# Last feed-forward rebuilt and interleaved with the second attention; its chunks on VectorE

## What is computed

```python
# second layer's attention (phasor memory), cut
ao = (gelu(off_in @ hop_w1 + hop_b1) @ hop_w2 + hop_b2).reshape(B, L, H, P + 1)
off_ph = center[:, :, :, None, :] + deltas[..., None] * 0.1
retrieved = (einsum('blpd,blhp->blhd', mem1_cos, qc) + einsum('blpd,blhp->blhd', mem1_sin, qs)) / sqrtP
gv = values[:, :, None, :] * gate[..., None]
kv_ret = (kv_cos * key_cos[..., None] + kv_sin * key_sin[..., None]).sum(axis=2)
# second layer's FFN: six experts of 64-64-64-64, the two best per token, weighted
rh = relu(features @ router_w1 + router_b1)
top_w, top_i = jax.lax.top_k(softmax(rh @ router_w2 + router_b2), 2)
routing_weights = softmax(top_w)
h1 = relu(einsum('bsd,edh->bseh', features, expert_w1) + expert_b1)
h2 = relu(einsum('bseh,ehf->bsef', h1, expert_w2) + expert_b2)
expert_out = einsum('bsef,efo->bseo', h2, expert_w3) + expert_b3
combined = sum over the two chosen experts of weight * expert_out
```

## Time and profile before

| | value |
|---|---|
| runs (us) | 1465.36, 1470.60, 1472.48; median 1470.6 |
| profiled execution | 1465.17 us, its span 1463.1 us |
| busy share PE / DVE / ACT / POOL | 80% / 60% / 42% / 42% |
| first attention | about 90 to 820 us |
| first FFN | about 820 to 940 us |
| second attention | about 950 to 1321 us |
| last FFN | 1321 to 1463 us |

### The profile page before, as it was taken

How to read it: one execution, slowest core, us unless ns; L and a number is a source line. 1 busy time by engine, 2 the same in 40 slices (tenths; PEclk the granted TensorE clock), 3 DMA queues, 4 the chain that set the end, 5 groups by cost and what they waited for, 6 DMA issues and landing times.

```text
span 1463.1 us, 26112 instructions
## 1 busy us (share of the span) xinstructions
PE 1167.1 (80%) x9805; PEld 769.0 (53%) x9805; DVE 875.2 (60%) x1807; ACT 614.5 (42%) x1249; POOL 608.9 (42%) x1193
## 2 busy tenths in 40 slices
PE   5579999999999999999999937305476674837995
PEld 3345565666666666666666623103264554734663
DVE  3434655655565565655656323146889888732998
ACT  1224555555554545545455413103352524213552
POOL 3201444734545445454554631478534635440000
PEclk9768999999999999999999967657667586666998
DMA  3100000000000000000000011211000000000000
GB/s 79 24 1 1 2 3 2 5 5 2 4 2 2 2 2 3 2 2 2 2 2 2 2 29 61 66 16 17 1 1 0 1 0 1 12 0 0 12 16 16
DMA packets 31369, 14.78 MB, mean 10 GB/s; under 512 B 27522, under 2 KB 28642, under 8 KB 31245
## 3 DMA queue, kind: packets, MB, share of 16 engines
q1 hardware_dynamic: 26637, 11.21, 3.3%
q0 software_dynamic: 4608, 1.91, 1.4%
HBM read 6.72 MB, written 7.27 MB: 10 GB/s over the span
## 4 chain that ended last, share of the span: by engine, by line
PE 63%; DVE 24%; POOL 6%; issue 4%; DMA 2%; ACT 1%; SPq 0%; POOLq 0%; DVEq 0%; ACTq 0%
PE psum L700 20%; PE psum L681 10%; PE psum L609 8%; PE psum L672 7%; PE psum L656 3%; DVE arena L1965 3%; PE psum L594 2%; DVE arena L1964 2%; DVE arena L1959 2%; PE psum L519 1%; POOL lnst L1089 1%; PE psum L614 1%; PE psum L751 1%; PE psum L764 1%; DVE lnst L1613 1%
## 5 line engine op out<-in xcount | busy, mean ns | idle before, releaser
L1355 ACT ACTIVATE arena<-psum 125x500 f32<-125x500 f32 x576 | 306.8, 585 | 342.9 <-PE psum L681 342.9
L1643 DVE TENSOR_REDUCE arena<-psum 125x1 f32<-125x500 f32 x384 | 242.6, 673 | 208.7 <-PE psum L609 208.5
L609 PE MATMUL psum<-arena 32*125 32x500 f32 (+1 forms) x1536 | 324.9, 520 | 0.6 <-ACT arena L1346 0.6
L700 PE MATMUL psum<-arena,XN 125*64 125x250 f32 x2304 | 308.6, 388 | 0.2 <-ACT arena L1355 0.2
L681 PE MATMUL psum<-arena 32*125 32x250 f32 x2304 | 293.9, 371 | 0.0
L681 PEld LDWEIGHTS psum<-arena 32*125 32x125 f32 x2304 | 216.0, 183 | 12.1 <-issue 1.4
L700 PEld LDWEIGHTS psum<-arena,XN 125*64 125x64 f32 x2304 | 140.6, 137 | 123.3 <-issue 78.0
L1646 DVE TENSOR_REDUCE arena<-psum 125x2 f32<-125x500 f32 x192 | 121.4, 674 | 72.6 <-PE psum L609 72.6
L609 PEld LDWEIGHTS psum<-arena 32*125 32x125 f32 x1536 | 128.6, 184 | 3.5 <-issue 2.1
L672 PE MATMUL psum<-arena,onesb 3*125 3x500 bf16 x576 | 123.3, 422 | 5.3 <-DMA arena<-arena 5.3
L1118 POOL TENSOR_SCALAR arena<-arena 125x4 bf16<-125x4 f32 x96 | 21.9, 229 | 217.3 <-DVE arena L1651 215.5
(11 more groups left out here) (327 smaller groups left out, 2079.0 us busy)
## 6 DMA issues: line engine op xcount, KB each, us to landing
arena<-arena SPq DMA_DIRECT2D x192, 1.5 KB
expert_in<-XN SPq DMA_DIRECT2D x8, 256.0 KB, 4.8
arena<-expert_in SPq DMA_DIRECT2D x4, 512.0 KB, 5.1
expert_out<-arena SPq DMA_DIRECT2D x4, 512.0 KB, 2.7
out<-H SPq DMA_DIRECT2D x8, 187.5 KB
expert_in<-XN,slot_in POOLq DMA_INDIRECT x48, 2.5
XN<-expert_out,slot_out POOLq DMA_INDIRECT x48, 3.9
arena<-in_L_ffn_w SPq DMA_DIRECT2D x2, 256.0 KB, 4.2
```

Source lines behind the costliest of these rows:

```text
L609: last = pe.matmul(ps[0:R, at_:at_ + hi - lo], QH[row:row + 32, b, g, j * R:(j + 1) * R], KH[row:row + 32, b, g, lo:hi], start=True, stop= ...
L700: last = pe.matmul(ctx_bank[64 * h2:64 * h2 + 64, 0:THIRD], XN[:, p, c, a, :], PR[:, x % 4, h2, i * THIRD:(i + 1) * THIRD], start=(c == 0) ...
L1355: act.activation(PR[:, x % 4, h2, :], st_bank[(2 * x + h2) % 3][0:R, 0:2 * THIRD], ACT.Exp)\
L1643: dve.reduce_max(MX[:, q % 2, 0, 2 * h2 + tile:2 * h2 + tile + 1], ps[0:R, 0:2 * THIRD], AX)\
```

## The change

It has five parts.

1. *The FFN by steps.* 24 steps k = (p, th, ep), both sequences in each. Layer 1 is two matmuls of 64 rows on the two halves of the array (`tile_position`), layer 2 two full ones. The gates are spread over partitions by a matmul with the 0/1 matrix `SEL` from transposed gates `GT`, and DVE multiplies the second layer's activations by them. Layer 3 has `e3w` as stationary operand, 64 output columns for each sequence, and sums all six experts in one bank together with the bias, weighted by the gates (`b3r`). ACT copies the sum, PE transposes it, DVE adds it to `H`; SP stores each half, 16 stores in place of 8.
2. *Its place.* `ffn_events` puts `router`, `logit`, `gates` of pair p into events 20, 21, 22 for p = 0, 26 to 28 for p = 1, 32 to 34 for p = 2, and two steps into each of events 23 to 25, 29 to 31 and 35 to 37. Pair 3's comes behind. Choices and routes are made for each pair, on 72 values of a partition in place of 288.
3. *Chunks on DVE.* POOL's part goes. DVE forms all four products in two instructions of 1024, then difference and sum, two halving additions in place of the two sums over heads, and the six of 128. ACT scales values and keys, eight instructions of 64 a chunk, after a new wait on `rg`; PE's wait on `ff` goes.
4. *First attention's start.* `before` now also holds the six scores of unit 1, and `max_step` is moved by three up to k = 11; the shift of unit 1 is at step 0.
5. *Small.* `room` is in event 16; POOL makes `SEL` and zeroes `GP`, `b3r` there; the broadcast of the third bias goes.

```diff
@@ plan
+        def ffn_events(x):
+            heads = 0
+            while head1 and heads < (1 if x is not None else 2):
+                kind, p = head1[0]
+                if x is not None and x <= NJ * (p + 1) + 13:
+                    break
+                events.append(head1.pop(0))
...
+            while body1 and (x is None or done < PER):
+                k = body1[0][1]
+                p = steps1[min(k, len(steps1) - 1)][0]
+                now = [g for g in given if g[0:2] == ("gates", p)]
+                if x is not None and (not now or now[0][2] == x):
+                    break
...
+            if EARLY:
+                ffn_events(x)
+        ffn_events(None)
@@ first attention
-            return (k - 3) // 2 if k < 15 else k - 9
+            return (k - 6) // 2 if k < 12 else k - 9
-        shift_at = {min(max_step(3 * q + 2) + 2, 3 * q - 1): q for q in range(1, NQ)}
+        shift_at = {min(max_step(3 * q + 2) + 2, 3 * q - 1) if q > 1 else 0: q for q in range(1, NQ)}
-        before += [("score", 0, i) for i in range(6)] + [("shift", 0)]
+        before += [("score", 0, i) for i in range(6)] + [("score", 1, i) for i in range(4)] + [("shift", 0)]
+        before += [("score", 1, i) for i in range(4, 6)]
@@ TensorE
+            def layer1(k):
+                for a in range(2):
+                    r = slice(64 * a, 64 * a + 64)
+                    ps, done = take(pe, ("l1", k, a))
+                    pe.matmul(ps[:, 0:HALF], e1w[r, ep, :], XT[r, cols], start=True, stop=True,
+                              tile_position=(64 * a, 0)).then_inc(done, 1)
+            def gate_spread(k):
+                emptied(pe, ("gt", p, th))
+                for a in range(2):
...
+                    pe.matmul(ps[:, 0:HALF], SEL[r, ep].rearrange("r e d -> r (e d)"),
+                              GT[r, p % 2, th * HALF:(th + 1) * HALF], start=True, stop=True,
+                              tile_position=(64 * a, 0)).then_inc(done, 1)
+            def layer2(k):
+                for a in range(2):
+                    emptied(pe, ("l1", k, a))
+                    ps, done = take(pe, ("l2", k, a))
+                    pe.matmul(ps[:, 0:HALF], e2w[:, ep, :], H1[(2 * k + a) % 4], start=True, stop=True)\
+                        .then_inc(done, 1)
+            def layer3(n):
...
+                for a in range(2):
+                    pe.matmul(ps[64 * a:64 * a + 64, 0:HALF], b3r[:, a, :], GT[:, p % 2, th * HALF:(th + 1) * HALF],
+                              start=True, stop=False, tile_position=(0, 64 * a))
+                for ep in range(3):
+                    for a in range(2):
+                        last = pe.matmul(ps[64 * a:64 * a + 64, 0:HALF], e3w[:, ep, :], H2[6 * (n % 2) + 2 * ep + a],
+                                         start=False, stop=(ep == 2), tile_position=(0, 64 * a))
+                elif kind == "step":
+                    if x < len(steps1):
+                        layer1(x)
+                    if 1 <= x <= len(steps1):
+                        gate_spread(x - 1)
+                        layer2(x - 1)
+                    if x >= 4 and x % 3 == 1:
+                        layer3(x // 3 - 1)
+                    if x >= 5 and x % 3 == 2:
+                        turned(x // 3 - 1)
@@ ScalarE, chunk
+                act.wait_ge(S["rg"], p + 1)
+                act.wait_ge(S["gate"], p + 1)
+                for n in range(4):
+                    v = CV[:, tiles.start + n // 2, n % 2, 1, :]
+                    act.activation(v, v, ACT.Copy, scale=GA[:, 0, 4 * q + n:4 * q + n + 1])
                 act.wait_ge(S["prod"], q + 1)
-                act.wait_ge(S["vsum"], q + 1)
+                for n in range(4):
...
+                                   ACT.Copy, scale=GA[:, 5, 4 * q + n:4 * q + n + 1])
@@ VectorE, chunk
+                for i in range(2):
+                    w = WA[:, i:i + 2, 16 * q:16 * q + 16].unsqueeze(3).to_broadcast([R, 2, 16, PP])
+                    last = dve.tensor_tensor(t4[:, 2 * i:2 * i + 2], cs, w, ALU.mult)
+                last.then_inc(S["prod"], 1)
                 dve.wait_ge(S["prod"], q + 1)
-                link(dve.tensor_tensor(p0, p0, p1, ALU.subtract))
-                dve.reduce_sum(UV[:, 0], PT[:, 0].rearrange("r g h p -> r g p h"), AX)
-                dve.wait_ge(S["vsum"], q + 1)
-                dve.reduce_sum(UV[:, 1], PT[:, 2].rearrange("r g h p -> r g p h"), AX).then_inc(S["uv"], 1)
+                dve.tensor_tensor(t4[:, 0], t4[:, 0], t4[:, 1], ALU.subtract)
+                link(dve.tensor_tensor(t4[:, 2], t4[:, 2], t4[:, 3], ALU.add))
+                h4 = PT.rearrange("r (n i) g h p -> r n i g (h p)", i=2)[:, :, 0]
+                link(dve.tensor_tensor(h4[:, :, :, 0:64], h4[:, :, :, 0:64], h4[:, :, :, 64:128], ALU.add))
+                link(dve.tensor_tensor(UV, h4[:, :, :, 0:32], h4[:, :, :, 32:64], ALU.add))
@@ VectorE, FFN
+            def gated(k):
...
+                for a in range(2):
+                    emptied(dve, ("l2", k, a))
+                    g, done = filled(dve, ("gate", k, a))
...
+                    dve.tensor_tensor(H2[6 * (n % 2) + 2 * ep + a], H2R[(2 * k + a) % 4], g[:, 0:HALF], ALU.mult)\
+                       .then_inc(done, 1)
```

More of the change, by code:

```diff
@@ L885, in product, with router @@
                     last.then_inc(done, 1)
+            def router(p):
+                if p == 0:
+                    pe.wait_ge(S["w_late"], 16 * 11)
+                for th in range(2):
+                    emptied(pe, ("xt", 3, p, th))
+                for th in range(2):
+                    cols = slice(p * L + th * HALF, p * L + (th + 1) * HALF)
+                    ps, done = take(pe, ("rh", p, th))
+                    pe.matmul(ps[0:64, 0:HALF], W["rw1"], XT[:, cols], start=True, stop=True).then_inc(done, 1)
@@ L887, in _, with turned @@
+            def turned(n):
+                emptied(pe, ("l3", n))
+                ps, done = take(pe, ("yt", n))
+                for m in range(3):
+                    last = pe.transpose(ps[0:R, m * 128:(m + 1) * 128], YS[:, n % 2, m * R:(m + 1) * R], ident)
+                last.then_inc(done, 1)
             for event in events:
@@ L904, in _ @@
                     product(event[2])
[L907 to L917, removed]
@@ L950, in _ @@
-            NX = len(units)
-            for x in range(NX + 1):
-                if x < NX:
-                    layer1(x)
-                if x:
-                    layer2(x - 1)
-                    if x >= 6 and x % 3 == 0:
-                        layer3(*units[x - 6][0:3])
-            layer3(*units[NX - 3][0:3])
+                elif kind == "router":
+                    router(x)
+                elif kind == "logit":
+                    logit(x)
+                elif kind == "gates":
+                    gates(x)
+                elif kind == "step":
[8 more added lines that the diff above has]
+                        turned(x // 3 - 1)
@@ L1797, in weights @@
             def weights(p):
[L1799 removed]
+                wa = [WA[:, i, 48 * p:48 * p + 48] for i in (0, 1, 3, 2)]
                 dve.wait_ge(S["wexp"], p + 1)
@@ L1972 @@
+                elif kind == "logit":
+                    choices(x)
+                elif kind == "gates":
+                    route(x)
+                elif kind == "step":
+                    if 1 <= x <= len(steps1):
+                        gated(x - 1)
+                    if x >= 5 and x % 3 == 2:
+                        added(x // 3 - 1)
 _INS = ['x', 'L0_tok_conv_w', 'L0_tok_conv_b', 'L0_tok_bn_gamma', 'L0_tok_bn_beta', 'L0_tok_bn_mean',
```

418 lines of the change are left out of this document (237 added, 181 removed).

## The result

The changed kernel takes 1428.2 us (median of four, 1425.6 to 1430.4) against 1471.5 for the kernel before on the same chip: ratio 0.971, 95% interval 0.968 to 0.975, 43 us less. The prediction was 1428.0, range 1388 to 1462. The profiled execution took 1428.26 with a span of 1426.3.

The account below looks back on a forecast made before the run. DVE was taken to bound the second attention and last feed-forward, nothing the tail between. From 1465.2 us, less 8 (start), 28 (chunks) and 5 (event 20 to the end), came 1424; plus 4 for the median, 1428, range 1388 to 1462.

Parts of the forecast that it names:

- The bound of each part: DVE bounds the second attention and old last feed-forward, nothing bounds the tail; PE bounds the new feed-forward.
- Chunks, -28: Second attention: chunks moved wholly to DVE take 6.4 us each; 33 us less, of which 28 is counted.
- Start, -8: First attention's start: removing the stall and slow steps saves 8 us, bounds 0 and 12, and carries through.
- A step on PE, 4.07: New feed-forward: a block of three steps takes PE 12.2 us with eight changeovers, 4.07 a step, 98 us in all.
- The clock behind a head, 3 each: Behind the attention: the clock needs 3 us to come back after each head.
- The parts of the end: Event 20 to the end: 54 us (events 20 to 25), 94 (26 to 37), 51 (pair 3), together 199.
- Interleaving buys little: Feed-forward steps among attention events: event 20 to the end takes 199 us instead of 204, 5 less.
- Heads, 14 each: Behind the attention: a pair's router, logits, choices, route and transposes take 14 us with PE nearly idle.
- Rival 1: Behind the attention: heads hide, their 28 us and 9 of clock fall to a third, chunk gives 33; 1398, chance 0.22.
- Rival 2: Second attention: DVE's relief isn't the path's; chunk gains 5 to 15 us, start nothing; about 1450, chance 0.15.
- Rival 3: Feed-forward steps: the clock stays low; at half clock 98 us double, 1506 if 80% of steps run low; chance 0.08.
- Rival 4: Feed-forward on PE: paired half-array matmuls don't overlap, 50 us more, 1478; chance 0.05.

Follow-up runs that it names:

- the run with the small additions: The changed kernel with GpSimd's residual, bias, scale and offset work done for one group of 64 columns instead of twelve: 1412.3 us, ratio 0.961.
- The last experiment: Against the 1412.2 us kernel (heads ahead of layer norms, steps spread, gates later), DVE makes the gates directly behind the choices: 1400.7 us, ratio 0.953.
- the kernel with two steps earlier: Against the 1414.9 us kernel (heads ahead of layer norms, steps one to an event beside heads), steps start two events earlier: 1423.3 us, ratio 0.968.

## Why the prediction was right, and where it wasn't

- **The bound of each part** held. DVE bounds the second attention: with the chunk alone, chunk 11 starts 28 us earlier. The wait of PE on a chunk's last instruction is 31.9 us, no longer 42.8; I had it under 40.
- **Chunks, -28.** The free chunk was put at 6.4 (the terms as given add up to 6.3) and is 6.25. From chunk 0 to chunk 11 after has 201.0 us, before 226.5 by 1032.82 and 1259.28: -25.5. The step that failed is "nothing waits for what stays": what stays on POOL holds DVE, 7.2 us in this stretch by the run with the small additions. Together that is 32.7, the 33 that I had counted before I took 5 off for a late PE; the allowance was near in size and wrong in cause. I expected first and third chunk alike; the first of pairs 1 to 3 are 9.1 to 11.5 against 6.25. And 4.5 us of the gain are given back by the clock some 13 us behind chunk 11, which the prediction had only as a general remark on PE.
- **Start, -8.** Some 20 us ahead of chunk 0, at the same instruction of DVE (L1787 in before, at 1014.06; L1921 in after, at 1005.50), after is 8.6 us ahead. At chunk 0 it is 7.4, and by the run with the old start 7 to 9. The third step starts at 102.80, in front of the 103 I named. "No 0.50 behind it" is true of what follows; the first slow stretch, ahead of it, lasts longer than before.
- **A step on PE, 4.07.** At full clock a block of three takes 1368.77 - 1356.37 less 0.73 for six transposes of the layer norm = 11.7 us, 3.9 a step. The Trainium skill (TensorEngine Tiling (Array Packing), Key Properties) has a change of tiling mode drain the engine, which I charged with 0.15 to 0.2 each. Without any charge 10.7 was the sum, with it 12.2. That 11.7 lies between is in part luck, since the price of a unit was too low and the charge too high. Two groups of row pairs, with no change between them, start 0.73 apart (1356.37, 1357.10), where I had 0.63 a pair. Two full products take 1.46 with a change behind them (1357.83 to 1359.29) and 1.37 with transposes of the same mode behind them (1363.42 to 1364.79). So the trace agrees that a change costs something, but no more than 0.09 us there. The three transposes take 0.42 instead of 0.64.
- **The clock behind a head, 3 each.** No row stood behind this term. The first step behind the transposes of pairs 1 to 3 takes 3.7 to 4.4 us (1308.71 to 1312.43, 1352.21 to 1356.37, 1389.10 to 1393.53) instead of 2.92 by the starts at 1312.43 and 1315.35, and the six transposes themselves 1.44 instead of 0.8: 1.5 to 2.2 us a head.
- **The parts of the end.** Event 20 to the end is 1426.3 - 1226.4 = 199.9 us; I had 199. Inside, 61 instead of 54 (events 20 to 25), 90 instead of 94, 48.6 instead of 51. That the sum is right to 1 us is luck. In the first part 34.6 us pass before the first step (I had 32) and 26.6 with the steps (I had 22). The clock has a share in it: it is 0.57 from 1240 to 1270, and I costed steps at full clock. PE also stands 9 us at the waits of head 0 (3.60 and 5.42). What each is worth no run shows.
- **"Interleaving buys little."** This step failed. It is worth 13.5 to 14.7 us, since the feed-forward behind everything is no faster than the old one (4 us slower by the traces). My sum held because I set new parts against the old total of 204, without asking what the rewritten feed-forward would be on its own. In the run with the old feed-forward event 20 to the end is 208.9 us, not 204: the 4.5 of the clock are in it. So the feed-forward's share is 9 to 11 instead of 5, and the chunk's is 22 to 25 instead of 28; these are the two errors that cancel, and that they do is luck.
- **Heads, 14 each.** Alone a head is 11.5 (pair 3), and 21.2 and 16.5 beside layer norms. The count of DVE's operations was right (25 in 6.3 us, I had 24 in 6.5). What was missing is what lies beside them. At head 1 ScalarE's ReLU stands behind two squares of the layer norm, which wait for DVE: the logits start 7.4 us behind the router instead of 2.2. The low clock adds 1.2 in the logits. And DVE's own part, from choices to gates, takes 9.5 us (1297.73 to 1307.21) instead of 6.3 at head 3, while POOL works on its wide instructions. That is 9.6 of the 9.7 us between heads 1 and 3. DVE at "a third or less" behind the attention was too low: 55 of 139 us, with the layer norms.
- **Rival 1, the heads hide (1398, 0.22).** Not in this kernel, as I argued, because the steps stand behind the gates in PE's order. The last experiment made them hide and reached 1400.7. Its price for hiding, 25 us, was near the 27 measured; the 5 us that it also counted from the chunk didn't come.
- **Rival 2 (1450)** needed the chunk to give 5 to 15. It gives 22 to 25.
- **Rival 3, the clock stays low,** is half true: not inside runs of steps, which have 0.99 to 1.00, but wherever attention and steps mix (0.57), and with two steps moved there the kernel is 8.4 us slower. The Trainium skill (TensorE: Matmul & The Clock Gate, A second HAM failure mode: psum-queue depth-cycling) has a kernel that cycles through the banks lose clock to short idle times between its groups of matmuls; the runs of steps here cycle all eight banks at 1.00 from 1400 on, so that isn't what is seen in them.
- **Rival 4** fell for the column pairs, 0.67 for two against 0.50 for one. The row pairs were not run apart; two of them take 0.73 by the starts, where a full product takes 0.68 to 0.73; that they overlap too is likely, but not shown.

## What to carry to other kernels

Work that leaves an engine frees more than its own time only if nothing of the same kind stays behind on it; look for what else runs there at the same instant. If several changes go in at once, cost each against a kernel that has the others: an interleaving is worth what it covers, even where the interleaved work is no faster. And a short serial chain between engines (choices, exponentials, gates) should be queued as early as its input is there, with its reader late. Moving the reader later by itself gained nothing here (1412.2 against 1414.9, the same ratio).

## What the runs showed of the hardware

- **DVE beside POOL is blocked by whole instructions.** DVE's products with two SBUF operands and 72 elements took 1.50 to 1.59 us beside POOL's of 768 elements (1.50 to 1.54 us) and 0.23 without; those of 512 elements 1.9 to 2.2 instead of 0.68. The copy of 72 elements, with one input, was held too, 1.55 against 0.20, and so was a TENSOR_SCALAR of 48, 2.14 against 0.45. A TENSOR_REDUCE was not: in head 1 of after it takes 0.23 at 1302.01, inside a POOL instruction of 1.54 us from 1301.97, and the TENSOR_TENSOR behind it takes 1.33. The Trainium skill (SBUF — State Buffer, SBUF: two separate sides) has the pair of ports that both use held for a whole instruction by whichever comes first, for DVE instructions with two SBUF inputs or in a two-port mode. The trace agrees, at one POOL instruction of 1.5 us for each DVE instruction: so small instructions are hurt most, and a chain of them should not lie beside POOL's wide ones.
- **A gain can be taken back by the clock.** The same 108 records took 16.40 us at a granted clock of 0.75 and 20.85 at 0.53, after the work ahead of them had been shortened.
- **The low level can persist under a full PE.** In the kernel with two steps earlier PE was busy 34.75 of 35 us at a mean of 0.65 (1255 to 1290), and all of 1255 to 1275 at 0.50. What raises it there was not tried.
- **A column half on its own is cheaper than a full product:** 0.50 us for 128 rows by 64 columns and 375 elements, where a pair of halves takes 0.67 and a full product, by its starts, 0.68 to 0.73 (1.37 and 1.46 for two).
